# A decoder layer on one core: the third norm of seven pairs on GpSimd instead of VectorE

## The reference

```python
x = _layernorm(x + _L0_attn_ref(x, Wq, Wk, Wv, Wo))      # q * cumsum(k * v), projected by Wo
x = _layernorm(x + _L0_xattn_ref(x, ctx_512, ctx_512))   # 32 query heads, 8 key heads, softmax
x = _layernorm(x + _L0_ffn_ref(x, ln_w, ln_b, W1, b1, W2, b2))

# inside _L0_ffn_ref, with x rounded to bf16:
h = mx_layernorm(x, ln_w, ln_b)      # (x - mu) * rsqrt(var + eps) * w + b, rounded to bf16
h = mx_linear(h, W1, b1)             # both operands quantised in blocks of 32 along the features
h = mx_gelu(h)
h = mx_linear(h, W2, b2)
return bf16_round(residual + h)
```

## Time and profile before

| | before |
|---|---|
| median of 3 runs | 300.63 us (300.57 to 300.79) |
| profiled execution | 300.56 us |
| its span | 298.8 us |
| TensorE busy | 271.9 us (91%), 1692 instructions |
| VectorE busy | 265.3 us (89%), 665 instructions |
| ScalarE busy | 222.8 us (75%), 364 instructions |
| GpSimd busy | 149.3 us (50%), 226 instructions |
| granted TensorE clock | 1.0 of full speed (2.4 GHz) over the span |

### The profile page before, as it was taken

How to read it: one execution, slowest core, us unless ns; L and a number is a source line. 1 busy time by engine, 2 the same in 40 slices (tenths; PEclk the granted TensorE clock), 3 DMA queues, 4 the chain that set the end, 5 groups by cost and what they waited for, 6 DMA issues and landing times.

```text
span 298.8 us, 5402 instructions
## 1 busy us (share of the span) xinstructions
PE 271.9 (91%) x1692; PEld 165.7 (55%) x1707; DVE 265.3 (89%) x665; ACT 222.8 (75%) x364; POOL 149.3 (50%) x226
## 2 busy tenths in 40 slices
PE   6898899989788999999999999999789988998887
PEld 2665467557536664677566756675346353534443
DVE  3899988998889989998999899989995999889993
ACT  4121376586888889998999899989988998875551
POOL 4828243164715647674767475735554344522321
DMA  6940033003013000201220112011000101000111
GB/s 220 386 103 5 0 71 98 12 12 89 0 29 105 0 2 7 56 2 46 67 59 1 45 64 60 2 41 53 17 1 2 35 1 36 2 2 0 37 35 37
DMA packets 13229, 13.74 MB, mean 46 GB/s; under 512 B 3464, under 2 KB 10504, under 8 KB 12936
## 3 DMA queue, kind: packets, MB, share of 16 engines
q1 hardware_dynamic: 12768, 12.60, 14.0%
q10 hardware_dynamic: 432, 0.79, 0.7%
HBM read 9.84 MB, written 2.10 MB: 40 GB/s over the span
## 4 chain that ended last, share of the span: by engine, by line
PE 51%; DVE 24%; ACT 14%; issue 6%; DMA 2%; POOL 2%; ACTq 0%; DVEq 0%; POOLq 0%
PE bank L2032 9%; PE bank L2072 8%; PE bank L2059 8%; DVE am L1339 5%; DVE nm L1252 4%; PE bank L1989 3%; PE bank L1963 3%; PE bank L2138 3%; ACT p_sb L835 3%; PE bank L2113 3%; DVE wam L1339 2%; ACT xT L828 2%; ACT y_sb L849 2%; PE bank L2111 2%; DMA p_sb<-in_wq 2%
## 5 line engine op out<-in xcount | busy, mean ns | idle before, releaser
L1252 DVE TENSOR_REDUCE nm<-bank 128x4 f32<-128x512 f32 x128 | 84.3, 681 | 9.8 <-PE bank L2032 9.3
L835 ACT ACTIVATE p_sb<-bank 128x512 f32<-128x512 f32 x128 | 71.9, 600 | 11.7 <-PE bank L2059 10.8
L2032 PE MATMUL bank<-kbd,xT 96*128 96x512 f32 x128 | 57.1, 462 | 5.8 <-DVE nm L1252 3.2
L2059 PE MATMUL bank<-xT,kbd 104*128 104x512 f32 x128 | 53.8, 441 | 2.9 <-ACT p_sb L835 1.7
L497 POOL TENSOR_SCALAR ve<-mv 128x2 f32<-128x2 f32 (+1 forms) x36 | 12.7, 352 | 65.6 <-DVE mv L1213 60.2
L2032 PEld LDWEIGHTS bank<-kbd,xT 96*128 96x128 f32 x128 | 23.8, 188 | 20.9 <-DVE nm L1252 11.0
L2059 PEld LDWEIGHTS bank<-xT,kbd 104*128 104x128 f32 x128 | 23.4, 189 | 18.5 <-ACT p_sb L835 11.6
L2072 PE MATMUL bank<-p_sb,va_sb 128*32 128x512 f32 x256 | 32.9, 602 | 0.1
L1339 DVE TENSOR_REDUCE am<-g_sb 128x32 f32<-128x1024 bf16 x16 | 30.3, 1895 | 0.9 <-ACT g_sb L855 0.9
L828 ACT ACTIVATE xT<-bank 8x1024 fp32r<-8x1024 bf16 x16 | 16.2, 1013 | 13.4 <-PE bank L2045 13.1
L504 POOL TENSOR_TENSOR rs<-ve,nhalf 128x2 f32<-128x2 f32 (+1 forms) x36 | 24.6, 684 | 3.0
(11 more groups left out here) (125 smaller groups left out, 595.2 us busy)
## 6 DMA issues: line engine op xcount, KB each, us to landing
xt_sb<-in_xt SPq DMA_DIRECT2D x8, 256.0 KB, 3.0
x_sb<-in_x SPq DMA_DIRECT2D x8, 256.0 KB, 2.9
out_dram<-o_sb SPq DMA_DIRECT2D x7, 256.0 KB, 2.2
k_sb<-in_ctx SPq DMA_DIRECT2D x8, 192.0 KB, 2.8
kbd<-k3r SPq DMA_DIRECT2D x28, 48.0 KB
x_all<-in_w SPq DMA_DIRECT2D x1, 1024.0 KB, 5.3
w_raw<-in_w SPq DMA_DIRECT2D x1, 1024.0 KB, 7.6
p_sb<-in_wkv ACTq DMA_DIRECT2D x2, 256.0 KB, 4.4
```

Of the source, the lines that this page charges most:

```text
L835: sc.activation(p_sb[:, k, :], bankB[k % 2][:, :], ACT.Exp, scale=SCORE_SCALE).then_inc(s_ex, 1)
L1252: ve.tensor_reduce(nm[:, b, u, g, :], bankA[(2 + k + 11 * b) % 2][:, :].rearrange("p (k t) -> p k t", k=KU), AX.X, ALU.max, negate=True).t ...
L2032: mm(bankA[(2 + k + 11 * b) % 2][:, :], xT[0:MR, b, u, g, :], kbd[p % 2][0:MR, b, u, :, :].rearrange("r k t -> r (k t)"), start=True, stop ...
L2059: mm(bankB[k % 2][:, :], kbd[p % 2][0:MR + 2 * KU, b, u, kk, :], xT[0:MR + 2 * KU, b, u, :, :].rearrange("r g s -> r (g s)"), start=True, ...
```

## The change

A new function `pair_norm3` on GpSimd computes what `norm3` computed on VectorE, with the same operands and result. It is called twice before `weight3`, for pair 0 in the head, pairs 1 to 4 in the loop body and pairs 5 and 6 in the tail; the calls of `norm3` for these pairs are gone from VectorE's list. Pair 7 keeps its two on VectorE. The new instructions wait for the rstd, for xb, and from pair 1 on for the weighting of the pair before, which read h0.

```diff
+            def pair_norm3(p, b):
+                pool.wait_ge(s_rs3, upto(p, b))
+                pool.wait_ge(s_xb, upto(p, b))
+                if later(p):
+                    pool.wait_ge(s_h1, PB * p)
+                hold(pool)
+                gp.tensor_scalar(h0_sb[:, b, :], batch_of(xb_all, p, b), mv3[:, b, 0:1], rs3[:, b:b + 1],
+                                 ALU.subtract, ALU.mult).then_inc(s_h0, 1)
...
                 if on[4]:
                     var_eps(p[4], mv3, ve3, s_mv3, s_ve3)
                     rstd(p[4], ve3, rs3, s_ve3, s_rs3)
+                    pair_norm3(p[4], 0)
+                    pair_norm3(p[4], 1)
                     weight3(p[4])
                     shift3(p[4])
...
                 quantise_weight(1, 3, 5)
-                norm3(0, 0)
                 denominators(1, 0)
                 quantise_weight(1, 0, 6)
-                norm3(0, 1)
                 quantise_weight(1, 1, 6)
...
-                if on[4]:
-                    norm3(p[4], 0)
-                    norm3(p[4], 1)
-                if on[3]:
                     maxima(p[3], 1, 6)
                     maxima(p[3], 1, 7)
...
                 max_low(6, 1)
-                norm3(5, 0)
-                norm3(5, 1)
                 maxima(7, 0, 0)
...
                 maxima(7, 1, 3)
-                norm3(6, 0)
-                norm3(6, 1)
                 maxima(7, 1, 4)
```

More of the change, by code:

```diff
@@ L651, in head @@
                 rstd(0, ve3, rs3, s_ve3, s_rs3)
+                pair_norm3(0, 0)
+                pair_norm3(0, 1)
                 weight3(0)
@@ L721, in tail @@
                 shift_product(3, mv4, rs4, nb4, s_rs4, s_nb4)
+                pair_norm3(5, 0)
+                pair_norm3(5, 1)
                 weight3(5)
@@ L738, in tail @@
                 shift(6, nb2, s_nb2)
+                pair_norm3(6, 0)
+                pair_norm3(6, 1)
                 weight3(6)
```

## The result

| | before | after |
|---|---|---|
| median | 300.71 us (4 runs, 300.57 to 300.85) | 318.65 us (4 runs, 316.94 to 319.37) |
| profiled execution | 300.56 us | 319.37 us |
| its span | 298.8 us | 317.6 us |

The changed kernel takes 1.0589 times as long (95% interval 1.0542 to 1.0636), 17.9 us more. The forecast was 300.4 us, with 301.4 as the upper end: wrong by 18 us.

The account below looks back on a forecast made before the run. In the steady passes the chain lies on TensorE, in the head on VectorE, then ScalarE's copy. Terms 4 x 0 + 0.05 + 0 - 0.25 = -0.2 us gave a 300.4 us median, range 299.6 to 301.4.

Parts of the forecast that it names:

- the price of the norm on GpSimd: Each moved 128x256 norm takes 0.40 us, on the line between 0.19 (2 elements) and 0.62 us (512 elements).
- The upper end of that price: 1.28 us a norm, 306 us in all; within rival D (norms of 0.8 us or more), chance 0.09.
- The lateness: At 1.28 us a norm, weighting 1.7 us late: 0.5 to 1.35 us on TensorE for each of six pairs.
- The slack: Steady passes: quantised h finished at 170.98, read by TensorE at 172.22, 1.24 us to cover a late h.
- I take 0.05: Tail, pair 5: a GpSimd norm may make the split wait, one norm of 0.4 us at most; 0.05 us taken.
- I take 0: Tail, pair 6: two 0.4 us norms fit GpSimd's mean wait of 1.6 us, h's quantisation doesn't move; 0 us.
- The steady passes: Loop, pairs 1 to 4: h ready at 167.7 instead of 167.82, which nobody can use; 0 us each, period 30.0 us.
- the wait for the q copy: Steady passes, VectorE: score maxima move forward, so its wait for ScalarE's q copy grows from 0.58 to about 1.3 us.
- The page's ratio: By 1.96 a norm takes 0.8 us, h 0.7 us late, 0 to 0.3 us a pass; rival D, chance 0.09.
- the step of 1.23 us: Head, VectorE at 79.41: small instruction waiting 1.06 us for GpSimd falls to 0.2 us; weight steps take 0.6 to 1.3 instead.
- the -0.25 taken for the head: Head, pair 0: worth -0.9 to +0.8 us as GpSimd and VectorE collisions shift; -0.25 us taken near the middle.
- the 0.88 that I had called the most: Head: TensorE's own work between its waits allows no more than 0.88 us of gain.

Follow-up runs that it names:

- the cheap form: Changed kernel with constants 1.0 and 0.0 in place of mean and rstd in the seven pairs' GpSimd norms (mult, add): 300.3 us against 300.76.
- the (add, mult) form: Changed kernel with GpSimd negating the mean first, then norming by (add, mult), for all seven pairs: 300.5 us against 300.53.
- pair 0 alone: Changed kernel with only pair 0's norms on GpSimd, in the (subtract, mult) form, the others on VectorE: 300.03 us against 300.76.
- The kernel that holds GpSimd: Changed kernel, but in the loop body GpSimd starts the residual addition only when VectorE has finished the quantised h: 309.31 us.
- The kernel with both aids: Changed kernel with GpSimd's residual addition held until quantised h is done (also pair 5), and filler matmuls ahead of TensorE's wait for h: 305.56 us.

## Why the prediction was wrong

- **The step that failed** is the price of the norm on GpSimd: "on the line between them 256 elements give 0.40 us, and I take that". It measured 1.24. The row that I interpolated (a tensor_scalar of 0.62 us for 512 elements) belongs to a (mult, add) with constants, the norm is a (subtract, mult); the two kinds are 2.7 times apart at equal size and constant operands (1.07 against 0.40). I had named the operands and the input type as the risk, and neither was it.
- **The upper end of that price was right** (1.28), but I gave all prices of 0.8 us and more 9 chances in 100, and the range left it out. For an operation that the trace does not show, the value taken and its upper bound were a factor of three apart; the nearest row by name was no ground for 91 to 9.
- **What follows from 1.28 us was also too small**: 306 us forecast, 318.65 measured. The lateness was priced well: 0.5 to 1.35 us a pass forecast, 0.9 measured. Missing were the 2.0 us of collisions, because the late quantisation leaves GpSimd's gap, and the 1.6 us of lower clock. I had used exactly this collision in the head and not asked for it in the passes. The slack was read a little too large as well: I took TensorE's read at 172.22 from the chain, the timeline has it at 172.06, which leaves 1.08 us and not 1.24. And the loss came in three passes, not four: pair 1 waits for nothing.
- **The tail.** "I take 0.05" for pair 5 looked at the split maxima only. TensorE already waited 0.65 us for the quantised h there, so nothing covered a delay; it is the dearest place, most of the tail's 5.5 us. "I take 0" for pair 6 was right about its h and missed the split maxima of pair 7: 1.0 us with the slow norms, nothing with the cheap or the (add, mult) form.
- **The steady passes, at 0.40 us**: right in the time. 300.3 us with the cheap form, and 1.22 us for one batch instead of two costs 0.6 us in all. One sign named for it did not come: the wait for the q copy did not grow from 0.58 to 1.3 us. It is 0.24 us in the cheap form. The 0.7 us freed on VectorE went into a wait of 0.44 us for TensorE's scores ahead of the last maxima, and the cast behind them takes 0.69 us instead of 0.22.
- **The page's ratio.** The Trainium skill (GPSIMD Engine Reference, section Performance versus the Vector engine) gives 1.96 between the engines, measured on a two-input addition. Here the same norm takes 0.408 us on VectorE and 1.235 on GpSimd, 3.0 times as long, and in the (add, mult) form 0.557 on GpSimd, 1.4 times. It warned in the right direction, and either form lies off it.
- **The head.** With norms of 0.40 us its steps came as described (weight steps held, the step of 1.23 us gone). In the changed kernel the 1.23 us stayed, since 2.6 us of norms put the weighting at 75.0, not 72.4. That still was a gain: this execution ran 0.84 us behind the one before at the 25th softmax piece, ahead of the head's norm, and 0.29 behind at the 33rd. With pair 0 alone the same stretch gains 0.6 us too; the weight step that had taken 1.03 us takes 0.41 in both. So the -0.25 taken for the head was the right sign and too small: 0.6 us with the slow norm, 0.7 with the (add, mult) form, and 1.1 with the cheap form, above the 0.88 that I had called the most. What is open: in the profiled executions of the cheap form and of pair 0 alone the passes behind lose that lead again, with two long periods between TensorE's reads of h in each (30.71 and 30.41 us; 30.40 and 30.42), although the second of these kernels has no moved norm in them.

## What to carry to other kernels

Price a moved operation by a row with the same pair of operations, and where there is none, give the whole span between the bounds a real chance or ask for the form that has a row. Before work moves onto the path between two engines, note what each of them does next: a delay beyond the slack is paid again when the delayed steps run into the other engine's work, and once more when TensorE's clock falls behind its wait. If a stall can't be removed, letting the delayed steps go first and filling TensorE's wait took back 13 of 18 us here.

## What was not expected of the hardware

- GpSimd's tensor_scalar on 128x256 with two per-partition operands: (mult, add) 0.55 us, (add, mult) 0.55, (mult, mult) 0.56; (subtract, mult) 1.22, (subtract, add) 1.22, (mult, subtract) 1.23, (add, add) 1.24. A single add, subtract or mult with one such operand takes 0.92 to 0.93 us. bf16 or f32 as input or output makes no difference (1.22 in each). The subtraction of a broadcast mean as tensor_tensor takes 0.61 us. In the slow form 64, 256 and 512 elements take 0.58, 1.22 and 2.07 us. Why the pairs differ was not tried.
- TensorE's granted clock fell to 0.50 for six microseconds behind a wait of 3.34 us, and to 0.62 and 0.81 behind 2.52 us; it stayed at 1.00 in the loop where the wait for h was 1.2 us with matmuls on zeros ahead of it.
- The kernel that holds GpSimd shows a dip that no norm explains, 0.50 between 220 and 224 us, before pair 5's; TensorE had been busy 2.83 of the 4 us ahead. It cost 1.9 us. The kernel with both aids shows no such dip in the same stretch, and what set it off is open.
